# Past state as 32x32 matmul tiles, seeded attention banks, and a new order of work on three engines

## The reference

```python
q, k, v = x @ Wq.T + bq, x @ Wk.T + bk, x @ Wv.T + bv     # x is layernorm(x_in)
q, k = elu(q) + 1, elu(k) + 1                             # 16 heads of 32 features
kv_cum = cumsum(einsum('bhtd,bhte->bhtde', k, v), axis=t)
numerator = einsum('bhtd,bhtde->bhte', q, kv_cum)
denominator = maximum(einsum('bhtd,bhtd->bht', q, cumsum(k, axis=t)), 1e-6)
attn = (numerator / denominator) @ Wo.T + bo
x1 = x_in + layernorm(attn)
z = layernorm(x1)
# per 32 elements: scale = max|z| / 7.5, then the nearest value of a 64-value grid; Wf the same way
out = x1 + layernorm(dequant(quant(z)) @ dequant(quant(Wf)).T + bf)
```

## Time and profile before

| | |
|---|---|
| median of 3 runs | 2616.3 us (2614.82 to 2617.29) |
| the profiled execution | 2617.22 us, of which 2615.4 us is the span from first to last instruction |
| TensorE | 2486.9 us busy, 95% |
| VectorE | 2149.4 us, 82% |
| ScalarE | 1138.5 us, 44% |
| GpSimd | 1054.9 us, 40% |
| DMA | 41 GB/s over the span |
| granted TensorE clock, mean | 0.994 of full speed |

### The profile page before, as it was taken

One profiled execution on the slowest core, in us unless ns is written; L12 is line 12 of the kernel. 1 busy time (PEld: TensorE's weight loads), 2 busy tenths in 40 slices (PEclk: granted clock), 3 DMA queues, 4 the chain that ended last, 5 costly groups with the idle time before them and its releaser, 6 DMA issues.

```text
span 2615.4 us, 62366 instructions
## 1 busy us (share of the span) xinstructions
PE 2486.9 (95%) x24082; PEld 2057.8 (79%) x24082; DVE 2149.4 (82%) x4177; ACT 1138.5 (44%) x2058; POOL 1054.9 (40%) x1482
## 2 busy tenths in 40 slices
PE   5999999999999999999999999999999999999996
PEld 4778878778778778788787787787787877877885
DVE  6788888888888888888888888888888888888885
ACT  4444444444444444444444444444444444444442
POOL 1344444344443334443344433444433344333433
PEclk8999999999999999999999999999999999999998
DMA  4011101111011111011111011110111110111100
GB/s 152 22 42 48 44 28 32 40 48 44 29 40 40 40 48 44 28 32 40 48 47 33 32 40 40 48 44 28 39 33 48 48 40 28 36 40 48 32 25 25
DMA packets 57483, 107.55 MB, mean 41 GB/s; under 512 B 6768, under 2 KB 7152, under 8 KB 56816
## 3 DMA queue, kind: packets, MB, share of 16 engines
q1 hardware_dynamic: 57456, 107.18, 12.8%
HBM read 73.60 MB, written 33.55 MB: 41 GB/s over the span
## 4 chain that ended last, share of the span: by engine, by line
PE 45%; DVE 37%; issue 11%; ACT 4%; POOL 2%; DVEq 1%; ACTq 0%; POOLq 0%; DMA 0%; SPq 0%
PE work L345 9%; PE work L347 8%; PE work L346 8%; DVE kc L832 6%; PE score L436 4%; PE work L362 4%; PE work L462 4%; DVE QT L813 3%; PE work L455 3%; DVE A L875 3%; DVE KT L813 3%; DVE bn_x L790 2%; DVE amax L900 2%; DVE bn_r L790 2%; DVE bn_f L790 2%
## 5 line engine op out<-in xcount | busy, mean ns | idle before, releaser
L875 DVE TENSOR_TENSOR A<-score,causal 128x512 f32<-128x512 f32 x512 | 317.5, 682 | 42.5 <-PE score L436 42.4
L599 ACT ACTIVATE o_buf<-x_res,shift_r,rs_r 128x512 f32<-128x512 f32 x128 | 104.4, 815 | 399.6 <-POOL shift_r L1050 399.6
L1057 POOL TENSOR_TENSOR x_res<-x_res,o_buf 128x512 f32<-128x512 f32 x128 | 178.7, 1396 | 209.5 <-ACT o_buf L599 209.5
L595 ACT CAST xT_hi<-work 128x512 fp32r<-128x512 f32 x128 | 74.6, 583 | 384.6 <-PE work L362 384.6
L345 PE MATMUL work<-wv_hi,xT_hi 128*128 128x512 f32 x512 | 215.3, 420 | 0.0
L345 PE MATMUL score<-xT_hi,wk_hi 128*128 128x512 f32 x512 | 206.1, 403 | 6.6 <-issue 6.6
L1047 POOL TENSOR_TENSOR rs_f<-ve_f,minus_half 128x1 f32<-128x1 f32 x128 | 70.2, 549 | 339.6 <-DVE ve_f L794 339.6
L345 PE MATMUL score<-xT_hi,wq_hi 128*128 128x512 f32 x512 | 206.7, 404 | 0.0
L345 PE MATMUL work<-wo_hi,oT_hi 128*128 128x512 f32 x512 | 203.3, 397 | 2.9 <-DVE oT_lo L882 2.6
L346 PE MATMUL work<-wv_lo,xT_hi 128*128 128x512 f32 x512 | 201.2, 393 | 0.0
L347 PE MATMUL work<-wv_hi,xT_lo 128*128 128x512 f32 x512 | 200.9, 392 | 0.0
(11 more groups left out here) (130 smaller groups left out, 6734.7 us busy)
## 6 DMA issues: line engine op xcount, KB each, us to landing
x_in<-in_x SPq DMA_DIRECT2D x128, 256.0 KB, 2.8
x_res<-in_x SPq DMA_DIRECT2D x128, 256.0 KB, 2.6
out<-f_buf SPq DMA_DIRECT2D x96, 256.0 KB, 2.0
out<-xd SPq DMA_DIRECT2D x32, 256.0 KB, 2.0
V<-in_wk SPq DMA_DIRECT2D x1, 1024.0 KB, 6.6
QT<-in_wq SPq DMA_DIRECT2D x1, 1024.0 KB, 7.6
kc<-in_wo SPq DMA_DIRECT2D x1, 1024.0 KB, 9.6
A<-in_wf SPq DMA_DIRECT2D x1, 1024.0 KB, 11.6
```

The lines of the kernel that those rows point to most:

```text
L875: nc.vector.tensor_tensor(A[:, j, :, :], score_bank[j][:], causal[:].unsqueeze(1).to_broadcast([P, G, P]), ALU.mult).then_inc(a_set, 1)
L1057: nc.gpsimd.tensor_tensor(x_res[:, b, :], x_res[:, b, :], o_buf[:, b % 2, :], ALU.add).then_inc(r_set, 1)
```

## The change

**Past state.** `S` is kept packed as [128, 4, 4, 32] (one 32x32 block per head). Instead of four 128x128 matmuls ahead of each sequence's attention there is one stage `past_products` per tile: 64 matmuls, each from a 32-row by 32-column tile of the array, with 128 columns streamed. Tile row is the head j in its group, tile column the group g, and head j's results go to bank `score[j]`. ScalarE copies the four banks to SBUF (`past`), and later writes each sequence's part into its attention bank before `attend` (`seed`), which now only accumulates. `scores(0)` waits for the copies. `att` always uses bank W2 and its wait for the bank moves from TensorE to ScalarE. The features of the attention result come out in another order, and `Wo` is laid out to match on the host.

**State.** One copy of the whole state bank per tile replaces sixteen small ones.

**Carried sums.** The copy of the last scan column into `KT` goes from VectorE to ScalarE (`carry`).

**Statistics and quantisation.** `stats` becomes `seen`, `join`, `widen`, and `quantise` becomes `greatest`, `scale`, `quantise`, so that other work can stand between the dependent steps. In the prologue all four `x_seen` stand ahead of the first `join`.

**Order.** On TensorE `v(0)` goes ahead of `denominators`, and `v(1)`, `v(2)`, `v(3)` go ahead of the attention of sequence 0; before, `v(2)` and `v(3)` stood inside the per-sequence groups. ScalarE, VectorE and POOL have their steps arranged anew; in the first turn the quantisation of Wf stands ahead of all else on VectorE but one bn_stats.

The core of the diff:

```diff
 BANK_ORDER = [
-    (("f", 2), W2), (("xd", 3), W1), (("den", 0), W0), (("v", 0), W2), (("kn", 0), W1), (("f", 3), W0),
-    (("v", 1), W1), (("x", 0), W2), (("att", 0), W0), (("kn", 1), W2),
-    (("v", 2), W1), (("o", 0), W2), (("x", 1), W0), (("att", 1), W1), (("kn", 2), W0),
-    (("v", 3), W2), (("o", 1), W0), (("x", 2), W1), (("att", 2), W2), (("kn", 3), W1),
-    (("x", 3), W0), (("o", 2), W1), (("att", 3), W0),
+    (("f", 2), W2), (("xd", 3), W1), (("v", 0), W0), (("den", 0), W2), (("kn", 0), W1), (("f", 3), W0),
+    (("v", 1), W1), (("v", 2), W2), (("v", 3), W0), (("x", 0), W1), (("att", 0), W2),
+    (("kn", 1), W0), (("o", 0), W1), (("x", 1), W0), (("att", 1), W2),
+    (("kn", 2), W1), (("o", 1), W0), (("x", 2), W1), (("att", 2), W2),
+    (("kn", 3), W0), (("x", 3), W1), (("o", 2), W0), (("att", 3), W2),
 ]
...
+                def past_products():
+                    if cur:
...
+                        wait_apart(pe, qn_set, count(i, 3))
+                        for b in range(NSEQ):
+                            for g in range(G):
+                                for j in range(HPG):
+                                    rows = slice(j * DH, (j + 1) * DH)
+                                    last = nc.tensor.matmul(score_bank[j][g * DH:(g + 1) * DH, b, :], S[rows, b, g, :],
+                                                            QT[rows, g, b * P:(b + 1) * P], start=True, stop=True)
+                        last.then_inc(past_mm, 1)
...
                 def attend(b):
                     if cur:
-                        take(i, ("att", b), here, before)
...
-                        for g in range(G):
-                            nc.tensor.matmul(att[:, g, :], S[:, b, g, :], QT[:, g, b * P:(b + 1) * P],
-                                             start=(g == 0), stop=False, skip_group_check=True)
                         pe.wait_ge(a_set, count(i, b * HPG + HPG - 1, 16))
                         pe.wait_ge(v_set, count(i, b))
+                        pe.wait_ge(seeded, count(i, b))
...
+                v(0)
                 denominators()
-                v(0)
                 kn(0)
+                f(3)
                 spread()
-                f(3)
+                v(1)
+                past_products()
+                v(2)
                 scores(0)
-                v(1)
+                v(3)
                 x_transposes(0)
                 attend(0)
                 state(0)
                 kn(1)
                 scores(1)
-                v(2)
                 if cur:
                     o(i, 0)
...
+                def carry(g):
+                    if cur:
+                        act.wait_ge(scanned, count(i, g))
+                        nc.scalar.copy(KT[:, g, :, CARRY], kc[:, g, :, SEG - 1]).then_inc(kc_set, 1)
...
+                def past(j):
+                    if cur:
+                        act.wait_ge(past_mm, count(i, 0, 1))
+                        nc.scalar.copy(past_att[:, :, j, :], score_bank[j][:]).then_inc(past_set, 1)
+
+                def seed(b):
+                    if cur:
+                        take(act, i, ("att", b), {0}, set())
...
+                        nc.scalar.copy(bank(("att", b))[:],
+                                       past_att[:, b, :, :].rearrange("p j t -> p (j t)")).then_inc(seeded, 1)
+
+                def state():
+                    if cur:
+                        act.wait_ge(st_mm, count(i, NSEQ - 1))
+                        nc.scalar.copy(S[:], state_bank[:]).then_inc(s_set, 1)
```

More of the change, by code:

```diff
@@ L259, in had_before, with take @@
             return None
+        def take(engine, i, stage, here, before):
+            found = had_before(stage, here, before)
+            if found is None:
+                return
+            other, turns = found
+            reader, per = freed[other[0]]
+            engine.wait_ge(reader, count(i + turns + tile_of(other), other[1], per))
         def tokens(t, g):
@@ L333, in _ @@
         def _(pe):
[L334 to L341, removed]
             def product3(dst, st_hi, st_lo, mv_hi, mv_lo):
@@ L396, in v @@
                     if cur:
-                        take(i, ("v", b), here, before)
+                        take(pe, i, ("v", b), here, before)
+                        if first and b == 0:
+                            pe.wait_ge(wf_lo_set, G)
                         weights(i, "v")
@@ L402, in denominators @@
                     if cur:
-                        take(i, ("den", 0), here, before)
+                        take(pe, i, ("den", 0), here, before)
                         if first:
-                            pe.wait_ge(wf_lo_set, G)
                             pe.wait_ge(small_loaded, 16 * N_SMALL)
@@ L469, in state @@
                         pe.wait_ge(kn_set, count(i, b))
[L470 to L473, removed]
+                        if b == 0 and not first:
+                            pe.wait_ge(s_set, count(i - 1, 0, 1))
                         for g in range(G):
@@ L483, in x_transposes @@
                     if nxt:
-                        take(i, ("x", b), here, before)
+                        take(pe, i, ("x", b), here, before)
                         pe.wait_ge(xn_set, count(i + 1, b))
@@ L488, in o @@
                 def o(tile, b):
-                    take(i, ("o", b), here, before)
+                    take(pe, i, ("o", b), here, before)
                     pe.wait_ge(oT_set, count(tile, b))
@@ L495, in xd_transposes @@
                     if prev:
-                        take(i, ("xd", b), here, before)
+                        take(pe, i, ("xd", b), here, before)
                         pe.wait_ge(xd_set, count(i - 1, b))
@@ L501, in f @@
                     if prev:
-                        take(i, ("f", b), here, before)
+                        take(pe, i, ("f", b), here, before)
                         pe.wait_ge(xdT_set, count(i - 1, b))
@@ L548, in turn @@
                 scores(2)
-                v(3)
                 if cur:
@@ L704, in turn @@
                     wf_high(3)
-                    selectors()
                 xd_hi(3)
+                kn(0)
+                f_norm(1)
+                for j in range(HPG):
+                    past(j)
+                seed(0)
                 if nxt:
                     x_norm(i + 1, 0)
-                kn(0)
                 f_norm(2)
@@ L828, in scan @@
                         dve.wait_ge(k_set, count(i, g))
-                        if first and g == 0:
+                        if not first:
+                            dve.wait_ge(kc_set, count(i - 1, g))
+                        elif g == 0:
                             dve.wait_ge(carry_zeroed, 1)
```

343 lines of the change are left out of this document (215 added, 128 removed).

## The result

The changed kernel takes 2653.45 us (median of 4 runs, 2651.8 to 2659.49), the kernel before 2616.16 beside it: a ratio of 1.0147, interval 1.0129 to 1.0165. It is 1.5% slower, where 2499 us was forecast. Almost every term of the sum can be found in the trace at the size it was given. The loss is something the sum had no term for.

The account below looks back on a forecast made before the run. TensorE was taken as the bound, 77.2 of a turn's 79.71 us being its own work. 30 looped turns at -3.74, the first at -4 and the last at -1.3 gave -117.5 us: 2499 us forecast, range 2476 to 2548.

Parts of the forecast that it names:

- the sum for a looped turn: TensorE's looped turn: 79.71 - 3.60 - 2.49 + 2.05 + 0.3 = 75.97 us, 3.74 less than before.
- The slower rival: Past-state matmuls: both passes of an fp32 matmul block the array, 5.9 us more a turn, 2688 us; chance 0.05.
- What leaves TensorE: Old past-state matmuls ahead of each attention go, saving 3.60 us a turn; waits at denominators and last attention go, saving 2.49.
- Both waits: TensorE's waits at the denominators (1.41 us) and the last sequence's attention and state (1.08 us) go: 2.49 us a turn.
- Past products: New TensorE stage of 128 passes in 32x32 tiles: 16 ns each, 2.05 us a turn, ends 12.8 and 35 ns.
- the first rival: Past-state stage: 32x32 passes go at 22 to 28 ns, giving 2524 to 2548 us; chance 0.17.
- the third: Past-state stage: paired fp32 passes block the array, from 45 ns a pass, 2688 us, slower than before; chance 0.05.
- 3.60 - 2.05 - 0.3: Per turn on TensorE: 3.60 us saved on old past-state matmuls, 2.05 for the new stage, 0.3 for tile-form switches.
- The covers: TensorE work hiding other engines' copies, divide, masks, splits and seeds in a turn: each holds by 0.4 to 3 us.
- the second rival: Per-sequence part: VectorE or ScalarE becomes the bound, 0.5 to 1.5 us a turn missed, 2515 to 2547 us; chance 0.13.
- The fourth: Order of work saves nothing because waits only move; only the new past-state passes gain, 2576 us; chance 0.03.
- First and last turn: Outside the looped turns: first k(0) 7.4 us later but turn 0 11 us shorter, together -4; last turn -1.3 us.

Follow-up runs that it names:

- the version with 125 increments: The changed kernel with 125 semaphore increments that nobody waits for ahead of TensorE's program, its loop body untouched: 2482.89 us, ratio 0.9487 to the kernel before.
- The straight one: The changed kernel with all 30 looped turns of TensorE's program written out, other engines still looping: 2467.02 us, ratio 0.9426 to the kernel before.

## Why the prediction was wrong, point by point

**The step that failed** is the sum for a looped turn, 75.97 us. It builds on "The other 77.2 us of the turn are TensorE's own work", which holds for the kernel before, and carries it to the changed one: the 64 new matmuls are costed by their time alone and their instructions never counted, and the jump at the turn's head is taken over at its 0.21 us of the earlier trace rows without a reason, though the change put 192 instructions into the body for the past products. A turn of 81.48 us against 75.36 without stalls: 6.12 us lost, 3.98 - 0.21 = 3.77 of them standing and the rest, 2.35, products at half clock. 29 x 6.12 = 177 us, and 2653.5 - 177 = 2476, the time of the kernel with two turns written out, at the lower end of the range given (2476 to 2548). None of the four rivals was this one. The slower rival had TensorE's passes in it, not their number of instructions, and all that is slower had a chance of 0.05.

**What leaves TensorE.** Both waits are gone as foretold. With the old products in the new order the turn is 1.94 us shorter, and that kernel has a new wait for ScalarE's normalised x, which the changed one has not:

```profile
PE work L365 <- ACT xn L603: 34.2, 34, 13.4
```

Less the 13.4 us of the start and some 5 in the first tile's other transposes this is 0.53 us a turn. So the two waits were worth 1.94 + 0.53 = 2.47 us, where 2.49 was given, if the rest of the new order costs and saves nothing, which was not measured apart.

**Past products:** 1.83 us, 14.3 ns a pass, where 16 was taken and 12.8 to 35 allowed. That refutes the first rival (22 to 28 ns) and the third (from 45 ns). It also speaks against the floor of 25 ns in the Trainium skill (page "TensorE: Matmul & The Clock Gate", section "Wait — 56ns, not 53.3ns?"; the prediction names the section ahead of it). Tiles for old products: 77.76 - 0.53 - 75.36 = 1.87 us saved, where 3.60 - 2.05 - 0.3 = 1.25 was given. Of the 0.62 between them 0.22 is the pace; the rest would be the 0.3 for switches of tile form and a tenth more, which I did not measure apart. The whole turn without stalls is 75.36, where 75.97 was forecast.

**The covers held.** Masks, seeds, past copies, divide and splits cause no TensorE wait in the looped turns, not even in the version with 125 increments, where no stall gives the other engines time: the second rival is refuted. The fourth is too, by 2467 us.

**First and last turn.** `k(0)` began at 26.71 us (26.1 foretold), and turn 0 took 98.15 - 26.71 = 71.4 us where it took 105.05 - 18.66 = 86.4; I had given it 11 us with 8 either way, it saved 15. With 0.6 us x 30 of the turn, and `k(0)` 0.6 late, this makes 21.4 of the 23 us by which the version with two turns written out lies below the 2499. The last turn to the end of the span took 1.7 us less there than before (117.6 against 119.3), where 1.3 was given. The straight one lies 9 lower still, and its turn is 0.28 us shorter.

## What to carry to other kernels

A loop is paid for in instructions, not only in time. Whoever adds matmuls to a loop on TensorE should count the body's instructions (four for each fp32 matmul, two for an fp32r one or a transpose) and look, in the profile before, at the head of the turn and at the packets of the instruction queue: a row of "issue" at the loop's head, with hundreds of packets, is a loop fetched anew in each turn. The cure costs nothing here: write the loop out on that engine, or move its begin by writing out turns, and look at the trace, since one turn written out left every jump stalling and two left none; and until then a version's time can change by 3 to 7% through any edit ahead of the loop, and two versions are compared only when neither stalls.

## What the runs showed of the hardware

- TensorE's instructions come in blocks of 256 (16.4 KB a packet), and a loop that lies across 7 blocks stays (no packet from 179 to 2496 us in the kernel before), one across 8 is fetched anew in each turn, by nine packets spread over it. The Trainium skill (page "Runtime: NRT & Kernel Launch", section "Instruction fetch mechanics") has blocks of 256 too, and the runs agree. It gives TensorE a buffer of 2048 instructions, which is 8 blocks; here 8 did not stay. That one block is being filled ahead is my reading; the ninth packet would fit it, and no run shows it. The same section says that a taken branch outside of a window of two blocks stalls; the kernel before jumps over 1547 instructions, 7 blocks, in 0.21 us and with no packet, against that.
- The stall goes with where in its block the target lies: 3.5 to 3.7 us at 234 instructions past a block's edge, 4.0 at 164, 4.8 to 5.0 at 68 and 91, 5.2 at 58 (these kernels differ in other things too), but 7.8 at 250, 6 instructions ahead of the next block. The last is two fetches in a row: in each of its 11 standstills two packets start within 0.7 us and a third 4.1 to 5.0 us later. A packet takes 0.9 to 2.5 us, and the first matmul starts 1.3 to 2.3 us after the last one has landed.
- 4 us without a matmul cost another 2.35 us: the granted clock is 0.50 in the 5.2 us behind it and 1.00 ahead of it, and `k(0)` takes 5.28 us in place of 2.86.
- 128 passes of 32x32 tiles, 128 columns each, start 14.3 ns apart.
